# Ternary feed-forwards: normed rows of sequences 1 to 7 split into fp16 halves in row layout and turned by DMA transposes

## The reference

```python
def _L1_ffn_ref(x, W1, b1, W2, b2):
    Wq1 = _quantize(W1)          # entries -1, 0, 1
    Wq2 = _quantize(W2)
    h = jax.nn.relu(jnp.einsum('bsd,fd->bsf', x, Wq1) + b1)   # 256 -> 1024
    return jnp.einsum('bsf,df->bsd', h, Wq2) + b2             # 1024 -> 256
...
x = x + 0.5 * _L1_ffn_ref(_layernorm(x, axis=-1), L1_ffn_W1, L1_ffn_b1, L1_ffn_W2, L1_ffn_b2)
```

## Time and profile before

| | before |
|---|---|
| median of 3 runs | 1905.88 us |
| span of the profiled execution, first to last instruction | 1904.6 us |
| PE busy | 1700.2 us, 89% |
| DVE, ACT, POOL busy | 1164.4, 857.4, 591.3 us |
| mean granted TensorE clock | 0.980 |
| first ternary sublayer, first up matmul to the attention's first matmul | 1353.62 to 1511.64 |
| second ternary sublayer, first up matmul to the end | 1766.49 to 1904.6 |

### The profile page before, as it was taken

The page is one execution under the profiler, slowest core; times in us unless marked ns, Lnnn a source line. Parts: engine busy times, 40 slices in busy tenths (PEclk is TensorE's granted clock), DMA queues, the critical chain, the costliest instruction groups (busy, mean ns, idle before and its releaser), DMA issues. The chain is left out here.

```text
span 1904.6 us, 42712 instructions
## 1 busy us (share of the span) xinstructions
PE 1700.2 (89%) x15082; PEld 1117.5 (59%) x15083; DVE 1164.4 (61%) x2413; ACT 857.4 (45%) x1479; POOL 591.3 (31%) x549
## 2 busy tenths in 40 slices
PE   1999989999879999998999989999688889899898
PEld 0556556666546666665556556665355657677466
DVE  5766775555446555555565555555576567576676
ACT  3444443333255554554333324343355455554664
POOL 0333230000334544213323210001687444343332
PEclk9999999999989999999999999999799999999999
DMA  7321122333221111001101023332223022121001
GB/s 268 86 77 62 62 93 85 98 99 98 52 34 23 22 33 28 6 1 40 43 31 43 24 89 100 99 99 72 55 51 55 0 69 69 36 69 36 12 33 45
DMA packets 98053, 114.31 MB, mean 60 GB/s; under 512 B 10736, under 2 KB 88592, under 8 KB 97296
## 3 DMA queue, kind: packets, MB, share of 16 engines
q1 hardware_dynamic: 79504, 79.02, 14.1%
q0 software_dynamic: 18432, 33.64, 7.2%
HBM read 64.26 MB, written 48.35 MB: 59 GB/s over the span
## 5 line engine op out<-in xcount | busy, mean ns | idle before, releaser
L1619 PE MATMUL ps<-xt_hi,wsh 128*128 128x512 f16 x512 | 195.3, 381 | 17.4 <-DVE aqkv_lo L1043 13.2
L1620 PE MATMUL ps<-xt_lo,wsh 128*128 128x512 f16 x512 | 195.2, 381 | 0.0
L1621 PE MATMUL ps<-xt_hi,wsh 128*128 128x512 f16 x512 | 195.0, 381 | 0.0
L1619 PE MATMUL ps<-later_hi,work 128*128 x576 | 187.8, 326 | 1.9
L1621 PE MATMUL ps<-later_hi,work 128*128 x576 | 187.6, 326 | 0.0
L1620 PE MATMUL ps<-later_lo,work 128*128 x576 | 187.6, 326 | 0.0
L809 ACT ACTIVATE work<-ps 128x512 f32<-128x512 f32 x128 | 76.4, 597 | 198.3 <-PE ps L1621 198.0
L614 POOL DMA_INDIRECT later_hi<-expert_y,gather_rows x64 | 89.2, 1394 | 232.9 <-issue 227.7
L614 POOL DMA_INDIRECT yg<-expert_y,gather_rows x64 | 81.4, 1272 | 245.2 <-issue 224.2
L1619 PE MATMUL ps<-wsh,work 128*128 128x256 f16 x512 | 141.9, 277 | 16.5 <-DVE work L1202 10.1
L1364 DVE SCALAR_TENSOR_TENSOR work<-ps,work 128x256 f32<-128x256 f32 x144 | 69.7, 484 | 131.1 <-ACT work L851 131.1
(11 more groups left out here) (261 smaller groups left out, 4378.4 us busy)
## 6 DMA issues: line engine op xcount, KB each, us to landing
work<-expert_x SPq DMA_DIRECT2D x144, 128.5 KB, 2.1
expert_y<-work SPq DMA_DIRECT2D x144, 128.0 KB, 1.9
yg<-in_w_later SPq DMA_DIRECT2D x16, 510.0 KB, 3.6
expert_x<-work SPq DMA_DIRECT2D x32, 128.5 KB, 3.5
values<-wsh SPq DMA_DIRECT2D x8, 512.0 KB, 3.2
later_hi<-values SPq DMA_DIRECT2D x16, 256.0 KB, 4.8
later_lo<-values SPq DMA_DIRECT2D x16, 256.0 KB, 4.7
out_x<-x SPq DMA_DIRECT2D x8, 512.0 KB, 2.9
```

Source lines behind the costliest of these rows:

```text
L1619: nc.tensor.matmul(out_, a[0], b[0], start=start, stop=False)
L1620: nc.tensor.matmul(out_, a[0], b[1], start=False, stop=False)
L1621: return nc.tensor.matmul(out_, a[1], b[0], start=False, stop=stop)
```

## The change

For sequences 1 to 7 of each ternary sublayer ACT (rows_hi_of) and DVE (rows_lo_of) split xn into fp16 halves in row layout, into xh, which lies in the space of wsh and has two buffers. rows_hi_of stands behind hi(5) in ACT's loop, rows_lo_of behind lo(7) in DVE's. SP then issues four DMA transposes, one for each tile of 128 tokens: 128 rows of 512 values (256 hi, 256 lo) become four 128x128 blocks of xt, which now holds both halves in one tensor. PE no longer turns these sequences; its up part waits for the DMAs. Sequence 0 of a sublayer, and the first sequence of the sublayer behind it, are turned by PE as before. ln_scale no longer waits for PE's transposes from the second step on. The skipped handovers are made up by increments of their semaphores. The stores of x are issued in the last sublayer's loop, each behind the transposes of the sequence two further on; the last two stand at the end.

```diff
-        xt_hi = sb("xt_hi", [P, 2, KT, XW], F16)
-        xt_lo = sb("xt_lo", [P, 2, KT, XW], F16)
+        xt = sb("xt", [P, 2, 2 * KT, XW], F16)
+        xt_hi, xt_lo = xt[:, :, 0:KT, :], xt[:, :, KT:2 * KT, :]
...
+        def rows_turned(n):
+            return SUBLAYERS[:n].count("l1ffn") * (NSEQ - 1)
...
+        xh = Carve(wsh)([2, TPS, 2 * D], F16)
...
+            def l1ffn(n):
+                s = S[n]
+                sp.wait_ge(x_updated, N0(n))
+                for g in range(1, NSEQ):
+                    if g >= 2:
+                        sp.wait_ge(s["up_ready"], (g - 1) * FU)
+                    sp.wait_ge(halves_lo_ready, rows_turned(n) + g)
+                    for t in range(TPS):
+                        sp.dma_start_transpose(xt[:, g % 2, :, PAD + t * P:PAD + (t + 1) * P], xh[:, g % 2, t, :]).then_inc(xt_in, 16)
+                    if n == len(SUBLAYERS) - 1 and g >= 2:
+                        store(g - 2)
...
+            for g in range(NSEQ - 2, NSEQ):
+                store(g)
             sp.wait_ge(x_stored, 16 * NSEQ)
...
+            def rows_hi_of(m, h, u):
+                act.wait_ge(xn_ready, m + 1)
+                nc.scalar.activation(xh[:, u, :, 0:D], xn[:, :, 0:D], ACT.Copy).then_inc(halves_hi_ready, 1)
...
                     for k in range(FU):
                         act.wait_ge(s["up_ready"], g * FU + k + 1)
+                        if is_first(g) and k == 0:
+                            act.sem_inc(xt_hi_ready, NSEQ - 1)
...
                         if k >= 1:
                             hi(k - 1)
+                        if k == 6 and not is_last(g):
+                            rows_hi_of(g + N0(n) + 1, rows_turned(n) + g + 1, 1 - u)
                     hi(FU - 1)
-                    xt_hi_of(g + N0(n) + 1, 1 - u)
+                    if is_last(g):
+                        xt_hi_of(g + N0(n) + 1, 1 - u)
...
+            def rows_lo_of(h, u):
+                dve.wait_ge(halves_hi_ready, h)
+                nc.vector.tensor_tensor(xh[:, u, :, D:2 * D], xn[:, :, 0:D], xh[:, u, :, 0:D], ALU.subtract).then_inc(halves_lo_ready, 1)
...
                     if down:
-                        down_part(g - 1, u, up)
-                    else:
-                        xt_lo_of(g + N0(n) + 1, 1 - u)
+                        down_part(g - 1, u, is_last(g))
...
                         if k == 4:
-                            ln_scale(g + N0(n) + 1, next_at(g))
+                            ln_scale(g + N0(n) + 1, next_at(g), first=not is_first(g))
+                        if k == 7 and not is_last(g):
+                            rows_lo_of(rows_turned(n) + g + 1, 1 - u)
...
                     if down:
-                        down_part(g - 1, 1 - u, up)
-                    else:
-                        transposes(g + N0(n) + 1)
-
-                def up_part(g, u):
-                    xt_ready(g + N0(n))
+                        down_part(g - 1, 1 - u, is_last(g))
+
+                def up_part(g, u):
+                    if is_first(g):
+                        xt_ready(N0(n))
+                        pe.sem_inc(pt_ready, NSEQ - 1)
+                    else:
+                        pe.wait_ge(xt_in, 16 * TPS * (rows_turned(n) + g))
```

More of the change, by code:

```diff
@@ L222, in build @@
         x_updated = sem("x_updated")
+        halves_hi_ready, halves_lo_ready = sem("normed_rows_hi_ready"), sem("normed_rows_lo_ready")
+        xt_in = sem("xt_transposed_by_dma")
         rstd_step = sem("rstd_step")
@@ L559, in win, with store @@
                     body(g, g % 2)
+            def l1ffn(n):
[9 more added lines that the diff above has]
+                        store(g - 2)
+            def store(g):
+                sp.wait_ge(x_updated, N0(len(SUBLAYERS) - 1) + g + 1)
+                sp.dma_start(od[:, g * TPS:(g + 1) * TPS, :], x[:, g * TPS:(g + 1) * TPS, :]).then_inc(x_stored, 16)
+            od = out.rearrange("(t p) d -> p t d", p=P)
             for n, kind in enumerate(SUBLAYERS):
@@ L563, in _ @@
                     ffn0(n)
+                if kind == "l1ffn":
+                    l1ffn(n)
                 if kind == "win":
                     win(n)
[L566 to L570, removed]
+            for g in range(NSEQ - 2, NSEQ):
+                store(g)
             sp.wait_ge(x_stored, 16 * NSEQ)
@@ L1402, in up_part @@
                         dve.wait_ge(s["h_hi_ready"], g * FU + k + 1)
+                        if is_first(g) and k == 0:
+                            dve.sem_inc(xt_lo_ready, NSEQ - 1)
                         nc.vector.tensor_tensor(h_lo[:, u, k, :], relu[:, k % RELUS, :], h_hi[:, u, k, :],
```

## The result

The changed kernel takes 2015.26 us (2013.64 to 2016.34, 4 runs) against 1904.43 us of the kernel before on the same chip: a ratio of 1.0575, 95% interval 1.0555 to 1.0595. 2020 was forecast, 1960 to 2118 the range. The profiled execution has a span of 2011.8 us, 107.2 more than before.

The account below looks back on a forecast made before the run. PE sets the pace in the second sublayer, POOL fills the first; the change adds a chain to each step. Second sublayer +7.9, +52.2, +1.7, first +7.2, +44.0, +1.7: +114.5 us on 1905.88 gives 2020 us, range 1960 to 2118.

Parts of the forecast that it names:

- One step of lead: Both ternary sublayers: the next sequence's operand is made one step ahead, leaving 4.47 us from ln_scale's end to the next up group.
- 4.75 us from ln_scale to the end of rows_lo: ACT and DVE queues: rows_hi, relu(7), hi(6), lo(6), lo(7) and rows_lo take 4.75 us after ln_scale ends.
- The clock, 1.7 us: PE after an idle wait: up starts at the 1.2 GHz level, adding 1.7 us to each step following an idle one.
- the 13.0: First sublayer, six steady steps: ln_scale ends 13.0 us after the step's first up matmul starts, before the slow clock is added.
- L = 7.0 us: Four DMA transposes: 1.97 us of issues, 4.7 to land, 0.3 for handovers; ends of the estimate 2.2 and 16.4 us.
- Steps of 24.69 and 26.45: Six steady steps each: 24.69 us in the second sublayer (+52.2 in all), 26.45 in the first (+44.0).
- POOL's 19.16: First sublayer: POOL's work repeats every 19.16 us, shorter than the forecast 26.45 us step and so hidden.
- (c): Rival, path from ln_scale to the next up group: under 4.47 us, PE stays the bound; faster, 1893 us; chance 0.04.
- (a): Rival, DMA transposes: short landing of 1.9 us, 4.2 us in all; +75 us, 1981 us; chance 0.15.
- (b): Rival, DMA transposes: slow transposing, 16.4 us a sequence; +246 us, 2152 us; chance 0.12.
- (e): Rival, whole kernel: small things cancel, time within 0.5% of the kernel before; chance 0.01.
- (d): Rival, DMA queue: moves single 2-byte elements, 262,144 packets and 0.66 ms a sequence, 11 ms in all; chance 0.02.

## Why the prediction was right

The forecast of 2020 us rested on a chain, and each link is in the trace.

**One step of lead.** Right, and what decides: in the second sublayer, the one where it was tried, two steps of lead turn the loss into a gain with the same DMAs.

**4.75 us from ln_scale to the end of rows_lo.** Measured 4.66. The new instructions cost what the evictions did (1.06 and 1.22 us against 1.02 and 1.21): reading SBUF rather than PSUM changed nothing.

**The clock, 1.7 us.** Right in both sublayers. In the second, T + 12.93 was forecast and measured. In the first, five of the six steady steps end ln_scale at T + 14.4. The sixth, from 1430.80, ends it at T + 14.02, because PE was back at 2.4 GHz 2.9 us into it, where the step from 1887.20 took 3.8. With PE kept at work by filler matmuls, a step of the first sublayer whose clock stayed up (T = 1485.23) ends it at T + 12.70:

```profile
1494.91 3.02 DVE L1125 TENSOR_SCALAR xn<-x,mv,rstd 128x256 f32 x4
```

So the slow start costs 1.7 us there too, and what was off is the 13.0 to which the forecast added it. That was one step of the kernel before, its shortest (17.49 us), taken for six. In it DVE lost 0.3 us between lo(0) and the statistics. The steps beside it name the cause, a wait for POOL's gathers: in two of the six steady ones it was 1.8 us and ln_scale ended at T + 14.7, as in the step from 1392.20:

```profile
1397.89 0.31 DVE L1103 TENSOR_SCALAR gather_rows<-expert_rows 128x8 int32 x1 [1.83 <-DMA later_hi<-expert_y,gather_rows]
```

In the longer steps of the changed kernel the gathers are early and this wait is gone. The forecast did not look at it; that it took the step in which the wait was least is luck.

**L = 7.0 us.** Measured 6.43 in the second sublayer. The sum was near, its parts were not: I took issues 0.65 apart and 4.7 us to land from the window reads of the earlier trace rows; it was 1.28 apart and 2.4 to land, 3.85 + 2.4 against 1.97 + 4.7. The two errors cancelled, so this term was right by luck. In the first sublayer it was 7.79 (1449.48 to 1457.27), and there the gathers were in the way, which I had costed at nothing, at most 2 us a step. The queues from 1449 to 1457.3 (packets, MB, share of 16 engines), and what the four transposes took to land:

```profile
q0 software_dynamic: 527, 0.66, 48.4%
q1 hardware_dynamic: 2176, 0.52, 31.6%
...
xt<-wsh SPq DMA_TRANSPOSE x4, 3.6
```

POOL's gathers hold 48% of the engines and landing takes 3.6 us instead of 2.4: 1.2 of the 1.36 us of difference. That it is the gathers, and not the sublayer, shows in its seventh step, during whose transposes POOL issues none. From 1529 to 1536:

```profile
q1 hardware_dynamic: 2176, 0.52, 33.3%
...
xt<-wsh SPq DMA_TRANSPOSE x4, 2.4
```

Landing is back at 2.4 us, and PE starts 6.37 us behind rows_lo (1529.62 to 1535.99).

**The sum.** Steps of 24.69 and 26.45 were forecast, 24.02 and 26.47 measured. The six steady steps of the first sublayer last 158.9 us against 158.7: ln_scale ends 0.3 earlier than forecast in most of them, rows_lo takes 0.1 less, the DMAs 0.8 more in four of them and 0.6 less in the last. For the second sublayer +61.7 was forecast and +57.4 measured, for the first +52.8 and +53.5: 114.5 against 110.8 us. Most of the 4.3 us by which the second is off is L, 0.6 too long in seven steps. POOL's 19.16 was hidden, as said.

**The rivals.** (c), PE still the bound, is excluded by the run without transposes. (a) and (b) were other sizes of L, 4.2 and 16.4; the measured 6.43 is below the forecast's 7.0, and 2.2 above (a). In landing (a) was nearer than the forecast, 1.9 against 4.7 where 2.4 was measured; what kept it out is the distance of the issues, 1.28 us and not 0.65. (e) is out by the size of the change. (d) is excluded by the 2,176 packets of q1 above for one sequence, 2,048 and one in sixteen more, instead of 262,144. What the Trainium skill states in "VectorE: DVE Perf Modes", section "The three transpose paths", 1309 ns for a 128x128 block by DMA, may not be multiplied by the blocks, as these traces show: sixteen blocks take 6.25 us from the first issue, 0.39 each, and in one instruction 3.7 us, 0.23 each. The advice of that page to use TensorE where its PSUM output is acceptable, which stands in its section "Rules for kernel authors", is borne out here for one step of lead; with two, in the second sublayer, the DMAs were the better place by 0.86 us a step. The 261 GB/s of the Trainium skill's "DMA: Bandwidth & Descriptors", section "Latency and other measured facts", are of the size of the bursts. DMA share in tenths and GB/s, 40 slices of 0.225 us from 1903 on:

```profile
DMA  0000000000000299000498000695000893006999
GB/s 0 0 0 0 0 0 0 0 0 0 0 0 0 68 282 224 8 0 0 110 286 185 2 0 0 162 290 131 1 0 2 208 289 83 0 0 237 350 355 346
```

Each transpose moves its 131 KB in a burst of some 0.6 us, about 220 GB/s on the mean and 282 to 290 in the best slice, and then the engines stand still until the burst of the next one, which comes one issue later (the last slices are the store). So in the second sublayer bandwidth was not the limit: of the 6.25 us, 3.85 are the issues of three transposes and 2.4 the landing of the fourth.

## What to carry to other kernels

Before work is taken off the busiest engine, measure the time between the moment its input is ready and the moment the next group needs it; if the new path is longer than that, the engine is relieved and the kernel is slower. The remedy that worked here is lead, one more step of it; the faster transfer and the better place of rows_lo together brought the loss from 5.75% to 2.0%, but no gain. In a chain, look at what stands in each in-order queue between a value and the handover: here two unrelated instructions ahead of rows_lo, and the wait of the first of them, cost 34 us. And where a step length is taken from a trace, look at all the steps: in the first sublayer those of the kernel before ran from 17.49 to 20.84 us.

## What the runs showed of the hardware

A DMA transpose has a price by the instruction on the issuing queue: 1.25 us for 128x256, 1.27 for 128x512, 1.64 for 128x2048 fp16 (medians), against 0.58 for a plain store of 512 KB beside it. A 128x512 one lands 2.4 us after its issue, a 128x2048 one 3.7, and a 128x512 one 3.6 beside a stream of gathers that holds 48% of the DMA engines; in the same sublayer, with the gathers over, it is 2.4 again.

Idle TensorE costs after the fact: 36 matmuls into a spare bank, 7.9 us of work with no use (1914.85 to 1922.78), made a steady step of the second sublayer 1.7 us shorter, because the next group then started at 2.4 GHz.
